# Second layer's first attention: the second batch's sixteen gathers moved behind the last quarter's modulation, three to a tile

## The reference

```python
for e in range(NUM_EXPERTS):                       # first layer, experts
    w_e = jnp.sum(weights * (indices == e), axis=-1, keepdims=True)
    h = jax.nn.gelu(xf @ w1[e] + b1[e], approximate=False)
    out = out + w_e * (h @ w2[e] + b2[e])
x = x + gb * out
h = _layernorm(x, axis=-1) * (1 + ca) + sa          # second layer
# attention, 16 heads of 64, 64 anchors
anchor_B = qk @ W_anchor.T * SCALE
attn = jax.nn.softmax(anchor_B, axis=-1)
s = jnp.sum(attn, axis=-2)
recip = jnp.where(jnp.isinf(s ** (-1.0)), 0.0, s ** (-1.0))
out = recip[..., None] * jnp.einsum('bhna,bhnd->bhad', attn, v)
out = jnp.einsum('bhna,bhad->bhnd', attn, out)
x = x + ga * (out @ W_out.T + b_out)
```

## Time and profile before

| | us |
|---|---|
| median of three runs (777.74, 779.26, 782.41) | 779.26 |
| the profiled execution | 780.26 |
| its span | 778.5 |
| first attention of the second layer, about | 310 to 372 |
| PE busy over the span | 654.1 (84%) |
| DVE busy | 570.3 (73%) |
| ACT busy | 400.4 (51%) |
| POOL busy | 277.6 (36%) |
| 64 gathers L652, busy | 63.3, mean 0.989 each |
| 28 additions L700, busy | 66.0, mean 2.357 each |
| chain of waits, share of PE / DVE / POOL | 58% / 21% / 7% |

### The profile page before, as it was taken

One profiled execution on the slowest core, in us unless ns is written; L12 is line 12 of the kernel. 1 busy time (PEld: TensorE's weight loads), 2 busy tenths in 40 slices (PEclk: granted clock), 3 DMA queues, 4 the chain that ended last, 5 costly groups with the idle time before them and its releaser, 6 DMA issues.

```text
span 778.5 us, 9648 instructions
## 1 busy us (share of the span) xinstructions
PE 654.1 (84%) x2985; PEld 470.0 (60%) x2985; DVE 570.3 (73%) x1441; ACT 400.4 (51%) x698; POOL 277.6 (36%) x229
## 2 busy tenths in 40 slices
PE   5777550399999995879989899899899899899897
PEld 2666540388878883446468555478555478556575
DVE  4889959279866736996976786866796866783763
ACT  3646233277777732334375444485443585442573
POOL 6457778200000026686202375211485120341100
PEclk9979755699999985989999999999999999999999
DMA  6441587778898610001000000000100000000000
GB/s 212 136 177 52 202 296 275 233 250 267 250 304 307 215 58 27 18 21 28 0 1 0 35 28 21 1 0 1 41 23 20 0 1 1 27 1 1 0 1 28
DMA packets 25779, 69.26 MB, mean 89 GB/s; under 512 B 5296, under 2 KB 8384, under 8 KB 24384
## 3 DMA queue, kind: packets, MB, share of 16 engines
q1 hardware_dynamic: 21632, 60.24, 23.0%
q0 software_dynamic: 4096, 8.40, 3.6%
HBM read 46.46 MB, written 22.16 MB: 88 GB/s over the span
## 4 chain that ended last, share of the span: by engine, by line
PE 58%; DVE 21%; POOL 7%; issue 6%; DMA 4%; ACT 4%; SPq 1%; DVEq 0%; ACTq 0%; POOLq 0%
PE ps L1685 14%; PE ps L1687 8%; PE ps L1681 8%; PE ps L1942 6%; PE ps L1689 6%; PE ps L1688 6%; DVE stats L1061 3%; POOL rows_by_expert L605 3%; PE ps L1960 2%; PE ps L1930 2%; DMA wbuf<-w_split 2%; DVE ring L1565 2%; DMA raw<-in_w 1%; DVE yb L1465 1%; DVE cmat L1641 1%
## 5 line engine op out<-in xcount | busy, mean ns | idle before, releaser
L652 POOL DMA_INDIRECT yb<-y_by_expert,ypos x64 | 63.3, 989 | 158.2 <-DMA y_by_expert<-ysb 142.6
L1685 PE MATMUL ps<-hid,fh 128*128 128x512 f32 x256 | 103.5, 404 | 5.1 <-DVE hid L1549 5.1
L1687 PE MATMUL ps<-hid,fh 128*128 128x512 f32 x256 | 101.4, 396 | 0.0
L605 POOL DMA_INDIRECT rows_by_expert<-h,pos x64 | 71.1, 1112 | 25.0 <-issue 18.9
L700 POOL TENSOR_TENSOR misc<-misc,ring 128x1024 f32<-128x1024 f32 x28 | 66.0, 2357 | 33.8 <-DVE ring L1539 28.7
L1549 DVE TENSOR_TENSOR hid<-ring,hid 128x512 fp32r<-128x512 f32 x56 | 38.6, 689 | 41.7 <-ACT hid L941 40.1
L1942 PE MATMUL ps<-ring,hn 128*128 128x512 f32 x112 | 56.5, 628 | 5.3 <-DVE ring L1539 5.3
L1685 PEld LDWEIGHTS ps<-hid,fh 128*128 128x128 f32 x256 | 48.2, 188 | 21.0 <-DVE hid L1549 10.3
L1960 PE MATMUL ps<-attnT,cmat 128*128 128x512 f32 x128 | 56.9, 592 | 0.0
L1687 PEld LDWEIGHTS ps<-hid,fh 128*128 128x128 f32 x256 | 48.3, 188 | 10.7
L998 ACT ACTIVATE ring<-ps 128x1024 f32<-128x1024 f32 x32 | 32.8, 1025 | 42.6 <-PE ps L1930 42.4
(11 more groups left out here) (326 smaller groups left out, 1702.4 us busy)
## 6 DMA issues: line engine op xcount, KB each, us to landing
wbuf<-w_split SPq DMA_DIRECT2D x46, 512.0 KB, 5.6
w_split<-parts SPq DMA_DIRECT2D x4, 2048.0 KB, 7.7
raw<-in_w SPq DMA_DIRECT2D x8, 512.0 KB, 8.5
xs<-rows_by_expert SPq DMA_DIRECT2D x16, 256.0 KB, 5.4
y_by_expert<-ysb SPq DMA_DIRECT2D x16, 256.0 KB, 4.5
ffn_raw<-in_ffn SPq DMA_DIRECT2D x1, 2816.0 KB, 11.1
rows_by_expert<-zeros SPq DMA_DIRECT2D x9, 256.0 KB, 2.5
xa<-in_x SPq DMA_DIRECT2D x4, 512.0 KB, 4.9
```

The source lines that it names most:

```text
L605: gp.indirect_dma_start(disp, bass.IndirectOffsetOnAxis(pos[:, b, k, t:t + 1].bitcast(U32), 0), h1[:, b % 2, t, :], None).then_inc(scatter ...
L652: gp.indirect_dma_start(yb[:, k, t, :], None, ydisp, bass.IndirectOffsetOnAxis(ypos[:, b, k, t:t + 1].bitcast(U32), 0))\
L1685: te.matmul(out_, w(0), x(0), start=first, stop=False)
L1687: return te.matmul(out_, w(0), x(1), start=False, stop=last_)
```

## The change

In the attention of the first batch (b == 0), no gather for the second batch is issued before tile 3. From tile 3 to 7, three are issued behind each addition, and the sixteenth behind the last three. The attentions of the other batches keep their order: two behind L685, two behind each addition of tiles 1 to 5, four behind the addition of tile 7. What each gather fetches, and where to, is the same.

```diff
                 if b == 0:
                     gather(0, places[14:16])
                     prepared(2, 0)
-                if more:
+                if b and more:
                     gather(b + 1, places[0:2])
                 for t in range(1, T):
                     pool.wait_ge(*dve_attn.now(t, b))
...
                     if b == 0 and t == 2:
                         modulate(3, 0)
-                    if more and t < T - 2:
+                    if b == 0 and t > 2:
+
+                        gather(1, places[3 * (t - 3):3 * (t - 2)])
+                    if b and more and t < T - 2:
                         gather(b + 1, places[2 * t:2 * t + 2])
                 if more:
-                    gather(b + 1, places[2 * (T - 2):])
+                    gather(b + 1, places[2 * (T - 2) if b else 3 * (T - 3):])
```

## The result

The changed kernel takes 784.53 us (median of six runs, 782.15 to 786.07) against 778.33 of the kernel before (six runs, 776.27 to 782.41). The ratio is 1.0069, interval 1.0042 to 1.0096. Measured again, in another set of runs, it was 1.0051, interval 1.0029 to 1.0073 (experiment e8). So it is slower, by 0.5 to 0.7%. The profiled execution takes 785.54 us, its span is 783.8, 5.3 more than before.

The account below looks back on a forecast made before the run. POOL was nearly full in the second layer's first attention. -2.35 + 0.75 + 0.75 + 3.30 - 0.30 = +2.15, with 1.0 for the clock +3.15: 783.4 profiled, 782.4 on the median's scale; range 778.4 to 784.7.

Parts of the forecast that it names:

- The sums 1 and 2 and the modulation: POOL's additions (L700) of tiles 1 and 2 start at 321.99 and 330.95; the last quarter's modulation ends at 335.7.
- The CAST of tile 4 gives the gain back: DVE's rounding CAST meets POOL's earlier addition of tile 2, ends at 333.35 instead of 331.55, delaying PE's transposes.
- Sum 4 2.35 earlier: POOL's addition of tile 4 runs 343.9 to 346.27, against 346.27 to 348.62 before.
- Three gathers where there were two, +0.75 a tile: Third gather meets DVE's next scaling, so the next addition starts at 3.75 instead of 3.00; tiles 5 and 6 pay.
- Three gathers where there were none, +3.30: Between POOL's additions of tiles 6 and 7: the latter starts 4.46 after the former ends instead of 1.16.
- The chain, +2.15: Sum of POOL's gains, delays and used-up cover up to PE's column sums: 2.15 us later, without the clock.
- The clock, +1.0 (bounds 0 and 1.7): PE idles 2.8 us before the column sums, falls to 1.2 GHz; column sums and first C products grow, 1.0 us.
- of three gaps in this attention: PE gaps of 2.01 and 1.68 brought half clock, 1.76 did not; so the longer 2.8 was taken to bring it.
- Within 0.5% as the likeliest class: Whole kernel's time changes by less than 3.9 us, what can be told from no change; chance 0.71.
- rival (3): Clock already falls in tiles 5 to 7, PE sets two of them at 1.07 each: +5.25, 784.5; chance 0.15.
- Rival (4): Gathers take no harm from a running scaling, the two long ones had another cause: +0.75, 780.0; chance 0.08.
- The strict reading of the Trainium skill: Two-input DVE instructions block only POOL operations reading SBUF, so a scaling stalls no gather; the trace was said to contradict it.

Follow-up runs that it names:

- e8: The changed kernel measured once more with no edit; ratio 1.0051, interval 1.0029 to 1.0073.
- e6: As e2, but modulation of the last quarter ahead of tile 2's addition, one gather behind tile 3's and seven at the end; ratio 0.9952.
- e2: Changed kernel with gathers re-placed: four behind tile 1's addition, two each behind tiles 3, 4 and 5, none behind 6, six at the end; ratio 0.9984.
- e7: e2 with seven needless PE products in the gap before the transposes of tile 4's maximum; ratio 0.9995.
- e5: Kernel before, with three gathers behind each of the additions of tiles 1 to 4 in the second and third attention, first untouched; ratio 1.0094.
- e4: Kernel before, with three of the first batch's four gathers behind tile 7's addition moved behind tile 6's; ratio 1.0117.
- e3: Changed kernel with five needless PE products between the first batch's last transposes and the wait for tile 7's addition; ratio 1.0021.

## Why the prediction was right or wrong

- *The sums 1 and 2 and the modulation:* right. Forecast 322.0, 330.95 and 335.7; measured 322.15, 330.97 and 335.68.
- *The CAST of tile 4 gives the gain back:* right, 1.96 us against "about 2", and PE's transposes of the last quarter at 338.45 against a forecast of 338.5. Part of this is luck. The 4.95 us from the maximum's transposes to the last quarter's were read in a stretch of low clock, and the forecast took them over without saying that the clock would have to fall again. It did, behind the gap of 3.35 us; in e8 it did not, and the last quarter's transposes stood 1.49 us earlier. e6 bears out that the CAST costs something: with the modulation ahead of sum 2 it is not held, and the combine starts 2.31 earlier than in e2 (-4.45 against -2.14), where sum 2 holds it. But 1.63 of these 2.31 are the clock, as e7 shows (-3.77, with e2's order and no low clock). That leaves 0.68, and e6 also has one gather less behind sum 3 than e2 and e7: this and the CAST were not told apart.
- *Sum 4 2.35 earlier:* right, 343.82 against 346.27, 2.45.
- *Three gathers where there were two, +0.75 a tile:* right, 0.77 (6.12 against 5.35), and again in e5.
- *Three gathers where there were none, +3.30:* right, 4.44 instead of 1.16 behind sum 6, 3.28; e4 alone gives 3.28 too.
- *The chain, +2.15:* right. The column sums start 2.11 later in absolute time (365.28 against 363.17), and e3, which takes the clock away, ends at +2.15.
- *The clock, +1.0 (bounds 0 and 1.7):* the fall was right, the size was wrong. It cost 3.0 (5.13 - 2.15). This is the term of the sum that was mis-sized, in three ways. I took the ratio 3.05 / 1.98 = 1.54 from products that ran only partly at the low clock (they start at 338.64, the clock falls at 339.2); the column sums grew by 3.57 / 1.84 = 1.94. Of the 1.5 us that my own 2.7 us and this ratio give, I took 1.0, without a reason; with 1.94 they would have given 2.5. And I said that what follows is DVE's: DVE waited 1.31 us before the first part of cmat, where it had waited 0.36, and 0.47 more between its parts, for products that took 5.18 instead of 3.70. Counted along the path, 1.73 us are lost up to the normalizer, 0.94 up to cmat and 0.44 in it.
- *The reading behind it,* "of three gaps in this attention": incomplete. There are others in the kernel before: one of 1.28 us, before 318.83, with no low clock behind it, and one of only 0.83, behind which the clock stood at 0.50 from 311.9 to 315.3. So "2.8 is longer than any gap shown" was no safe ground for the fall:

```profile
311.80 0.72 PE L1685 MATMUL ps<-anch,hTa 128*128 128x512 f32 x1 [0.83 <-DVE hTa L1504]
```

- *Within 0.5% as the likeliest class:* that followed from the mis-sized term. +3.15 lies under the bound of 3.9, +5.2 over it. The median of 784.53 lies just inside the range, and that is luck: the forecast of 782.4 was 2.1 too low, its own upper bound ended at 784.2, and only the price of rival (3), which did not happen, carried the range to 784.7. The sign that cmat would be 2 to 3 us late failed as well, for the same reason: L1644 starts at 370.87, 4.8 later than L1641 did (366.09). (The floor of the bounds adds up to 26.4 and not 26.3, which changes nothing.)
- *Rival (3),* with +5.25 nearly the measured number, is still not what happened: the clock in tiles 5 to 7 stayed at 1.00. The number came from a longer low clock at the end. In e3 the clock did fall in tile 6, and the sums did not move by it, so its price of 1.07 for each such stretch was not found either.
- *Rival (4)* is out. The gathers that started under a running scaling took 1.84, 1.07, 1.07 and 1.76 us in the changed kernel and 1.08 in e5, against 0.95, each ending some 0.8 after the scaling. A gather that is already under way when the scaling starts is another matter: in the changed kernel neither of the two is longer for it.

```profile
347.59 0.95 POOL L652 DMA_INDIRECT yb<-y_by_expert,ypos  x1 [0.30 <-issue]
```

```profile
347.88 1.23 DVE L1542 TENSOR_TENSOR ring<-ring,lrec 128x1024 f32<-128x1024 f32 x1
```

- *The strict reading of the Trainium skill,* SBUF — State Buffer, section "SBUF: two separate sides", by which a scaling with two inputs would stall no gather, does not agree with these rows. The gathers of this kernel take their row numbers from `ypos`, which lies in SBUF. If that counts as a read by POOL, the section's sentence on two inputs does forecast a stall; no run here separates the two readings. That section's other statement, that the later of the two is blocked for the whole instruction of the first, is what every long CAST here shows (333.35 against a sum's end of 333.31, for one); the gather at 347.59 and the scaling at 347.88 do not show it.

## What to carry to other kernels

Before work is moved to a quieter place, count what cover that place has: here a loop of two engines that hold each other up had 0.64 us of room a tile beside two gathers, the third cost 0.77 each time, and behind the last addition but one there were 1.16 us, less than the 1.76 that a single gather took there. An engine made free earlier starts its next instruction earlier, and that instruction may then stand in the way of a short one on the other engine; look at what it will meet there, and change the order of the two if need be. And a new gap on PE must be priced with the low clock behind it, over everything that PE does on the path until it has recovered: 3.0 us here, against the 1.0 of the forecast. It is a risk and not a certainty, for the same gap brought it in one execution and not in another.

## What I had not expected of the hardware

A gap on PE of 2.84 us was followed by 6.8 us at 1.2 GHz, from 364.9 to 371.7, though PE worked without a pause from 365.28 on; in e8 it came 1.5 us after the work had begun again and also lasted 6.8 us (363.0 to 369.9), and in e4, behind 2.85, from 389.0 to 395.8. The length of a gap alone does not tell what follows it. Those of 2.01 and 1.68 us in the kernel before were followed by 3.4 us at 1.2 GHz each, that of 3.35 in the changed kernel by 3.4, that of 3.38 in e2 by 6.8, one of 0.83 in the kernel before and one of 0.65 in e3 by 3.4, but those of 1.76 in the kernel before and of 3.34 in e8 by none. Filling a gap with 2.3 us of needless products kept 2.4 GHz in e3, where the three executions with the gap open had lost it; 3.2 us of them in e7 went with 2.4 GHz too, but there e8 had kept it without them.
